# Gate and up products of two tiles at once by Strassen's scheme in a gated cross-attention block

## What is computed

```
x = x + tanh(g_xattn) * attention(q=layernorm(x), k=v=ctx)      # one head, softmax over 77 keys, biases bq, bv, bo
n = layernorm(x)
gate, up = fp4(n) @ fp4(w_gate).T, fp4(n) @ fp4(w_up).T          # 512 -> 1408 each
x = x + tanh(g_ffn) * (fp4(silu(gate) * up) @ fp4(w_down).T)     # 1408 -> 512
```

## Time and profile before

| | us |
|---|---|
| median of 3 executions (832.07 to 834.51) | 834.1 |
| the profiled execution, first to last instruction (span) | 832.3 |
| PE busy | 822.4 |
| DVE busy | 650.7 |
| ACT busy | 459.9 |
| POOL busy | 400.5 |

### The profile page before, as it was taken

One profiled execution on the slowest core, in us unless ns is written; L12 is line 12 of the kernel. 1 busy time (PEld: TensorE's weight loads), 2 busy tenths in 40 slices (PEclk: granted clock), 3 DMA queues, 4 the chain that ended last, 5 costly groups with the idle time before them and its releaser, 6 DMA issues.

```text
span 832.3 us, 11653 instructions
## 1 busy us (share of the span) xinstructions
PE 822.4 (99%) x4102; PEld 417.0 (50%) x4102; DVE 650.7 (78%) x967; ACT 459.9 (55%) x930; POOL 400.5 (48%) x333
## 2 busy tenths in 40 slices
PE   9999999999999999999999999999999999999998
PEld 5555445444554445444544454445544454444445
DVE  5887899898998698877878688778876878776654
ACT  2778675547555666456563755366646565344320
POOL 3498797764334353444333543454444533444421
PEclk9999999999999999999999999999999999999999
DMA  9723703553243434532641255224433443222232
GB/s 318 285 70 103 157 13 97 122 128 92 48 80 106 108 82 89 129 56 54 114 120 40 55 110 136 61 60 99 97 61 61 85 85 73 58 54 55 48 75 73
DMA packets 192817, 78.21 MB, mean 94 GB/s; under 512 B 176387, under 2 KB 178037, under 8 KB 192759
## 3 DMA queue, kind: packets, MB, share of 16 engines
q1 hardware_dynamic: 192759, 77.47, 39.6%
HBM read 22.76 MB, written 8.39 MB: 37 GB/s over the span
## 4 chain that ended last, share of the span: by engine, by line
PE 93%; ACT 3%; DVE 2%; issue 1%; DMA 1%; POOL 1%; POOLq 0%; ACTq 0%; DVEq 0%
PE banks L1918 60%; PE banks L2037 27%; DVE banks L1417 1%; PE banks L2053 1%; PE banks L1912 1%; PE banks L1971 1%; PE banks L1999 1%; PE banks L1998 1%; PE banks L2143 1%; DMA x_T<-x_parts 1%; PE banks L2150 0%; PE banks L2008 0%; PE banks L2160 0%; PE banks L2165 0%; PE banks L2155 0%
## 5 line engine op out<-in xcount | busy, mean ns | idle before, releaser
L1918 PE MATMUL banks<-wgu_hi,x_T 128*128 128x512 f16 (+1 forms) x1536 | 439.3, 361 | 1.6 <-DMA x_T<-x_parts 0.9
L1918 PE MATMUL banks<-wgu_lo,x_T 128*128 128x512 f16 (+1 forms) x768 | 277.5, 361 | 0.0
L1918 PEld LDWEIGHTS banks<-wgu_hi,x_T 128*128 128x128 f16 x1536 | 150.3, 98 | 155.6 <-issue 1.3
L2037 PE MATMUL banks<-wd,arena 128*128 128x512 f16 x1023 | 227.2, 379 | 0.0
L2037 PEld LDWEIGHTS banks<-wd,arena 128*128 128x128 f16 x1023 | 99.7, 98 | 117.4 <-issue 0.6
L648 POOL TENSOR_TENSOR arena<-arena,h_r 128x1024 f32<-128x1024 f32 (+1 forms) x60 | 93.2, 1554 | 115.3 <-DVE h_r L1372 115.3
L648 POOL TENSOR_TENSOR arena<-arena,h_s 128x1024 f32<-128x1024 f32 x64 | 90.7, 1418 | 88.6 <-DVE arena L1419 53.6
L1918 PEld LDWEIGHTS banks<-wgu_lo,x_T 128*128 128x128 f16 x768 | 75.1, 98 | 76.8 <-issue 0.3
L648 POOL TENSOR_TENSOR xwork<-xwork,x_s 128x512 f32<-128x512 f32 x32 | 38.4, 1201 | 152.0 <-DVE xwork L1419 152.0
L1052 ACT ACTIVATE arena<-banks,scal 128x512 f32<-128x512 f32 (+1 forms) x96 | 61.9, 647 | 84.9 <-PE banks L1918 84.8
L1571 DVE SCALAR_TENSOR_TENSOR arena<-arena,scal,banks 128x512 f32<-128x512 f32 (+1 forms) x90 | 62.2, 694 | 56.3 <-PE banks L1918 53.5
(11 more groups left out here) (199 smaller groups left out, 1043.6 us busy)
## 6 DMA issues: line engine op xcount, KB each, us to landing
ring<-in_x_dram SPq DMA_DIRECT2D x8, 1024.0 KB, 5.1
out_dram<-ring SPq DMA_DIRECT2D x31, 256.0 KB, 2.2
arena<-in_L_ffn_w_down_dram SPq DMA_DIRECT2D x4, 704.0 KB, 5.0
arena<-in_L_ffn_w_gate_dram SPq DMA_DIRECT2D x5, 512.0 KB, 9.7
arena<-in_L_ffn_w_up_dram SPq DMA_DIRECT2D x5, 512.0 KB, 9.6
ring<-in_L_xattn_Wk_dram SPq DMA_DIRECT2D x4, 256.0 KB, 6.1
ring<-in_L_xattn_Wq_dram SPq DMA_DIRECT2D x4, 256.0 KB, 6.8
wd<-in_ctx_dram SPq DMA_DIRECT2D x1, 1024.0 KB
```

The lines of the kernel that those rows point to most:

```text
L1918: ended = e.matmul(at, l, r, start=(i == 0), stop=(i == len(terms) - 1))
L2037: ended = e.matmul(by_k(down_ps(t)[:, :], KD), l, r, start=(k == 0 and i == 0), stop=(k == KH - 1 and i == 2))
```

## The change

From tile 8 on (`FIRST` = 4, so pair 4), two tiles u = 2q and v = 2q + 1 are worked as one pair q. The input parts of the pair (two tiles by two halves of the inner dimension) and the weights (gate and up, by two halves of the inner dimension) form two 2 by 2 block matrices, and the four products of the first two chunks are made by Strassen's scheme in Winograd's form: seven products `p1` to `p7` of 6 matmuls of 512 columns each, where the plain way takes eight. The third chunk (384 columns) stays plain: `rest(q, t, m)`.

The scheme needs sums of inputs and sums of weights. The sums of inputs are made once a pair by POOL (`px_sums`, four subtractions or additions of 256 columns), split into parts by ACT (`ps_high`) and DVE (`ps_low`) and transposed by two more DMAs (`su_turn`, `sv_turn`). The sums of weights are made once, during tiles 4 to 7, by PE with identity and negated identity matrices (`t_sum`, `t4_sum`: 48 matmuls of 512 columns), and split by ACT (`t_high`, `t4_high`) and DVE (`t_low`, `t4_low`). Partial results are shared: ACT copies the first product from bank 0 to bank 1 (`p1_copy`) and the seventh from bank 3 to SBUF (`p7_copy`), DVE adds (`c_begin`, `up_v`), and PE goes on accumulating in the banks that they wrote.

The norm and quantization of x are done for both tiles of a pair in instructions of 1024 columns (`px_stats`, `px_apply`, `px_scales` and so on), one pair ahead. The hidden row is quantized in place in three buffers, where there were two and two work tiles. From batch 3 on ACT writes the key bias into the score banks (`bias_write`), PE adds the scores to it with three matmuls of 77 columns per slice, the exponential reads PSUM and gives its sum, so that three DVE instructions over the scores go. The values go through a DRAM buffer (`v_park`) and are loaded a batch at a time; x has 3 ring slots. For tiles 30 and 31 the parts of h are 512 and 896 columns. The lists of the start and of tiles 0 to 7 are in a new order.

The core of the new loop on PE, and the functions it calls:

```diff
-            for t in range(7, NT):
-                gate_up(t, 0, 0)
...
-                down(t - 2, 2)
+            set_banks()
+            for q in range(FIRST, LAST_PAIR):
+                on(q, 1, att_values, 2)
+                on(q, 1, att_values, 3)
+                p1(q, 0)
+                p7(q, 0)
+                p6(q, 0)
+                p2(q, 0)
+                p5(q, 0)
+                p4(q, 0)
+                p1(q, 1)
+                on(q, 0, att_scores, 0)
+                p3(q, 0)
+                p7(q, 1)
+                on(q, 0, att_scores, 1)
+                down(2 * q - 2, 0)
+                p6(q, 1)
+                down(2 * q - 2, 1)
+                on(q, 0, att_scores, 2)
+                p2(q, 1)
+                p5(q, 1)
+                on(q, 0, att_scores, 3)
+                p4(q, 1)
+                down(2 * q - 2, 2)
+                p3(q, 1)
+                rest(q, 0, 0)
+                rest(q, 0, 1)
+                rest(q, 1, 0)
+                rest(q, 1, 1)
+                down(2 * q - 1, 0)
+                down(2 * q - 1, 1)
+                on(q, 0, att_values, 0)
+                on(q, 0, att_values, 1)
+                down(2 * q - 1, 2)
+            def pair_product(to, x_of, w_of, first):
+                (hi, lo), (w_hi, w_lo) = x_of, w_of
+                for k in range(K2):
+                    for i, (l, r) in enumerate([(hi[k], w_hi[k]), (hi[k], w_lo[k]), (lo[k], w_hi[k])]):
+                        ended = e.matmul(by_k(to, BANK // P), l, r, start=(first and k == 0 and i == 0), stop=(k == K2 - 1 and i == 2),
+                                         skip_group_check=True)
+                return ended
+            def p6(q, c):
+                w.wait_ge(su_turned, 16 * (q - FIRST + 1))
+                w.wait_ge(p1_copied, WHOLE * (q - FIRST) + c + 1)
+                pair_product(SUM_B, s_half(0, 0), w_sum(c, 2), False).then_inc(p6_mm, 1)
+            def p5(q, c):
+                w.wait_ge(c_begun, WHOLE * (q - FIRST) + c + 1)
+                pair_product(SUM_B, s_half(1, 1), w_sum(c, 1), False).then_inc(p5_mm, 1)
+            def p3(q, c):
+                w.wait_ge(up_v_made, WHOLE * (q - FIRST) + c + 1)
+                pair_product(SUM_B, s_half(0, 1), w_half(1, c, 1), False).then_inc(up_mm, 1)
```

The scores from batch 3 on:

```diff
-                        e.matmul(bank[at][:, c:c + 2 * KEYS], xn_T[i % 2][:, k, :], key_parts(b, k), start=(k == 0), stop=False)
-                        ended = e.matmul(bank[at][:, c:c + KEYS], xn_T[i % 2][:, KD + k, :], key_parts(b, k)[:, 0:KEYS], start=False, stop=(k == KD - 1))
+                        for l, m in ((hi, keys[0]), (hi, keys[1]), (lo, keys[0])):
+                            ended = e.matmul(to, l, m, start=False, stop=(k == KD - 1 and l is lo), skip_group_check=True)
```

The new instructions between the products of a pair, and the sums of the inputs:

```diff
+            def p1_copy(q, c):
+                n = WHOLE * (q - FIRST) + c
+                w.wait_ge(p1_mm, n + 1)
+                w.wait_ge(h_made, OLD + NCH * (q - FIRST) + c)
+                e.copy(SUM_B, SUM_A).then_inc(p1_copied, 1)
+            def c_begin(q, c):
...
+                e.tensor_tensor(SUM_C, SUM_B, h_of(2 * q)[:, c * BANK:(c + 1) * BANK], ALU.add).then_inc(c_begun, 1)
+            def up_v(q, c):
...
+                e.tensor_tensor(h_of(2 * q + 1)[:, cols], SUM_B, h_of(2 * q)[:, cols], ALU.add).then_inc(up_v_made, 1)
+            def px_sums(q):
...
+                e.tensor_tensor(v1, v0, v1, ALU.add).then_inc(*step())
...
+                e.tensor_tensor(v0, u0, v0, ALU.subtract).then_inc(*step())
...
+                e.tensor_tensor(u0, v1, u0, ALU.subtract).then_inc(*step())
...
+                e.tensor_tensor(u1, u1, u0, ALU.subtract).then_inc(ps_made, 1)
```

1596 lines of the change are left out of this document (1001 added, 595 removed).

## The result

The changed kernel takes 842.7 us (median of 6 runs, 838.3 to 846.7), the kernel before 833.6 us in the runs beside it: the ratio is 1.0111, 95% interval 1.0078 to 1.0144. The forecast was 827 with a range of 816 to 839, faster. It is slower by 1.1%, outside the range. The runs of the changed kernel lie in two groups, near 838.5 and near 846, and the median falls between them; the profiled one took 839.7 us, its span is 837.8. The groups are part of the explanation.

The account below looks back on a forecast made before the run. PE was taken as the bound, time being a count of matmul columns. Terms -20.3 + 5.5 + 1 + 2 - 1 + 6 = -6.8 us on the 832.3 span gave 825.5; with 1.8 for the median, 827, range 816 to 839.

Parts of the forecast that it names:

- PE alone: PE's matmul columns over the 12 pairs: 31.1 us less from fewer products, 10.8 more for weight sums; -20.3 us.
- pair waits: In the pairs, p6 waits for p1_copy and p3 for up_v, 0.5 us a pair, 11 pairs: +5.5 us (0 to 18).
- tiles 0 to 7: Forecast for tiles 4 to 7: splitting the weight sums adds 12 us to DVE, 11 to ACT, and fits; +1 (0 to 4).
- passage: Passage to pairs: p7 of pair 4 waits for x summed and transposed, ps_low being late on DVE; +2 us (0 to 5).
- start: Start, with lists in a new order: earlier waits of 6.7 us bound the gain; -1 us (-5 to +4).
- end: End: hidden-row chains of tiles 30 and 31 outlast PE's cover, waits of 4.7 and 1.8 us; +6 (3 to 8).
- the clock: Rival, 3%: PE's clock falls in the new waits, 12 matmuls after p6's wait at half rate, 31 us in all; 852 us.
- a wait before the last full down product: Sign in the profile after: one PE wait of 4 to 5 us there, from the transposing DMA.
- PE reaches tile 8 more than 5 us from 10.8 later: Alarm sign: the forecast is wrong if PE's arrival at tile 8 is that far from 10.8 us later than before.
- The handoffs: Rival, 20%: handoffs fit, no waits in the pairs, 4 us at the end; -15.3 us, 819 us.
- Blocking by DVE and POOL: Rival, 27% (12 same, 15 slower): in the pairs they block each other, PE waits 2.0 us a pair; +9.7, 844 us.
- PE might not get the columns back: Rival left out of the chances: products accumulating on banks written by ACT and DVE could run slower; no size given.

Follow-up runs that it names:

- b1_start: The changed kernel with ScalarE's start reordered, copies that PE waits for ahead of statistics, squares and folds; 835.0 us, 1.0023 to the kernel before.
- a2_fill: The changed kernel with matmuls that nobody reads before its two longest PE waits (key product 3, down product of tile 30); 839.7 us, 1.0078.
- c3_all_fill: c1_all with 22 matmuls that nobody reads in front of the down product of tile 30; 831.0 us, 0.9975 to the kernel before.
- a4_stats: The changed kernel with px_stats moved behind p1_copy and p7_copy in ScalarE's list of a pair; 856.0 us, 1.0274.
- b2_pairs: The changed kernel with px_stats cut in two, sums in front of p1_copy and squares right behind it; 843.5 us, 1.0115.
- c0_changed: The changed kernel itself, run again as the measure for others; 846.0 us, 1.0143 to the kernel before.
- c1_all: The changed kernel with mended orders of start, tile 3, passage and pairs together, plus su_turn and pair 4's p1_copy earlier; 831.0 us, 0.9978.
- a3_end: The changed kernel with PE's end reordered and, by a slip, finish of tile 28 behind the scales of tile 31; 849.8 us, 1.0188.
- d1_start: c1_all with more ScalarE copies moved up: three gu_high casts in the start and two more items in the pairs; 831.4 us, 0.9978.
- d2_end: d1_start with the end also reordered on four engines; 831.5 us, 0.9976 to the kernel before.

## Why the prediction was wrong, by its own steps

By the profiled executions, the span grew by 5.5 us where the sum said -6.8:

| term | forecast | measured | from |
|---|---|---|---|
| PE alone | -20.3 | -20.3 | 1008 matmuls at 0.216; four tiles 5.10 us shorter, 5.18 by columns |
| pair waits | +5.5 | +5.8 | five of 0.87, one of 0.79, one of 0.70 |
| tiles 0 to 7 | +1 | +2.8 | 190.2 us against 176.6, less 10.8 of sums |
| passage | +2 | +3.6 | waits of 2.3, 0.5 and 0.8 |
| start | -1 | +4.9 | first gate matmul 113.3 against 108.4 |
| end | +6 | +8.1 | 25.5 us against 24.5 less 7.1 |

The measured terms add up to +4.9; 0.6 is in no term. The sum missed the span's change by 12.3 us, and the start alone is 5.9 of them, the end 2.1, tiles 0 to 7 1.8, the passage 1.6, the pairs 0.3. The median, 842.7, lies 3 us further off through the group near 846.

*The step that failed first is the start.* "The waits there add up to 6.7 us before, nothing of it can fall by more" (they are ten, not nine) bounded the gain by rows and guessed the loss from the largest wait. The order of ACT in the start was at hand, and walking through it as I did through a pair would have shown `key_copy(1)` behind 6.7 us of work that nobody waits for, with PE's product free to use it 3 us earlier. b1_start shows it: with that order mended the median falls by 7.7 us (3.5 against the group near 838.5), and in its trace the first gate matmul comes 3.3 us earlier, of the 4.9 that were lost.

*The second is the clock, which I gave 3%.* I looked for it in the pairs' waits of 0.9 us, where it never fell. It fell in or behind waits of 2.1 to 4.8 us in the start, at tile 3, in the passage (in some executions) and at the end, where my own sum had put a wait of 4.7. The earlier trace rows show a clock of 1.00, but the longest wait behind them is 1.5 us: they could not speak against it, and I let them. In the profiled span 13.6 us are at half, for the first 1.0 of which PE was idle: some 6.3 us of PE's time, 2.9 in the start, 1.7 at tile 3; the 1.7 at the end cost nothing (a2_fill, c3_all_fill). In the group near 846 the start loses 5 to 7 us more, waits and clock together. The Trainium skill (TensorE: Matmul & The Clock Gate, "A second HAM failure mode: psum-queue depth-cycling") tells of idle times that make the clock swing; the prediction cited it and then weighed it by the pairs alone. The traces agree that idle time of PE is what precedes a fall (46 falls, each in or behind a wait), but not behind short and frequent ones: it was single waits of 1.9 us and more. The 852 us of this rival also leave out the pair waits behind which the clock would fall; with the sum's 5.5 it would be 858.

*The end: right mechanism, too small.* Tile 30's chain was forecast at 17.0 us and a wait of 4.7; it is 17.15 and 5.0. Tile 31's was forecast at 14.9 and is 16.4 from the last up matmul's end: `L1707` over 512 columns, 0.7 alone, takes 2.08 beside POOL, and POOL's divides 1.8 and 2.0 where they take 1.1 and 1.7 alone. (4.7 and 1.8 are 6.5, which the sum took as 6; measured are waits of 5.0 and 1.4 and 1.7 of clock.) The sum covers a last tile's chain as if it ran alone, but a pair ends both its tiles at once, and the two chains share DVE, ACT and POOL.

*The pairs were right*, in size (42.35 us a pair against 42.1) and place: p6 on `p1_copy`, 0.87 in even pairs, within the forecast's 0.1 to 1.4. p3's wait for `up_v` was 0, the low end, since `up_v` was done at 8.9 to 9.7 us, not at 9.9 to 10.5; a4_stats shows that this cover was thin. The rounding rows of 1024 columns are as forecast (1.22 us). The tell-tale signs "a wait before the last full down product" and "about 2 in down_last" were right (4.8; 1.2). PE's busy time (808.5, not near 802) and its idle time (29 us, not near 20) were not. "PE reaches tile 8 more than 5 us from 10.8 later" held as the alarm: it came 18.5 later.

*The rivals.* The handoffs did not all fit. Blocking by DVE and POOL said 844, near what was measured, from 2.0 us of wait a pair; PE waited 0.5, so that the number fits is luck. Its mechanism is in the trace all the same, in the place that the forecast named. In each pair one rounding of 384 columns takes 0.55 us and the other 1.76 (1133 ns on average), beside a product of POOL. At the end of pair 5, on POOL, DVE and ACT:
```profile
385.43 2.85 POOL L752 TENSOR_TENSOR arena<-arena,h_s 128x1024 f32<-128x1024 f32 x1 [2.42 <-DVE arena L1707]
```
```profile
386.92 1.76 DVE L1705 SCALAR_TENSOR_TENSOR arena<-arena 128x384 f32<-128x384 bf16 x1
```
```profile
390.23 0.51 ACT L1226 CAST h_parts<-arena 128x384 f16<-128x384 f32 x1 [0.88 <-POOL arena L752]
```
ACT is idle for 0.88 us in front of the last `h_high`, waiting for POOL's product over those 384 columns, which waits for this rounding; then come the statistics, the copy, and p6 with its 0.87. By an estimate from these rows, a rounding of 0.55 us there would bring the copy up to 0.88 us forward and take the wait of the even pairs away; in odd ones the two value products cover the same delay. No run here tested it: a4_stats and b2_pairs took the statistics out of the way instead. So the two engines' blocking had a share in the +5.8 of the pairs, and with `x_low(3)` and the last tile's chain one outside them, but not the 22 us of the rival. The Trainium skill (SBUF — State Buffer, "Terms") says that the one that finds the shared port pair taken waits for the other's whole instruction; the 2.19 us of `x_low(3)` agree, which end 0.55 after POOL's 1.93. That PE might not get the columns back is refuted by the 5.10 us.

Open stay what lengthens the start's waits in one execution and not in the other, and why the clock fell behind the wait of 2.3 us at tile 3 in the changed kernel and not behind the 2.2 of c0_changed.

## What to carry to other kernels

When a change rewrites the order of an in-order engine, walk through every stretch where it is new, the start and the end too, not only the loop: ask of each copy that the bound engine waits for what stands ahead of it that nobody waits for. Price a wait of a busy PE by what the clock takes behind it too, and look whether something else waits anyway before counting that as a gain; filling a wait with matmuls that nobody reads won some 2 us where PE was the bound and nothing where it was not. Expect a mended wait to uncover the next link of the same chain: the moves gathered in c1_all gave 11.7 us against the changed kernel by the medians (8.7 by the profiled spans), the best of the seven kernels tried behind it 2.1 more.

## What the runs showed of the hardware

The granted clock went to 0.50 (1.2 GHz) for 3.41 us at a time, for 6.83, or once, in a3_end, where PE had waited 8.6 us, for 10.24. Over the 18 profiled executions of the changed kernel and its variants it fell in, or up to 1.4 us behind, 31 of 32 waits of PE of 2.6 us or more, 13 of 24 of 2.0 to 2.3 us, and two of 1.9 us (d1_start and d2_end, at 86 us); behind the many of 1.6 us and less it never fell. Where PE had matmuls in such a wait it stayed at 1.00, five times of five; the same two places without them saw it fall 21 times of 21.

A DVE instruction with two SBUF inputs took 2.19 us beside a product of POOL where it takes 0.68 otherwise (`x_low(3)`), and a rounding of 384 columns 1.76 where it takes 0.55.
